# Summing the per-partition counts of a bisection by a round trip through HBM instead of a TensorE product

## Chip, core and metric

One NeuronCore of one Trainium2 chip runs the whole program in one launch. The metric is the device time in microseconds (us); lower is better. The core has five instruction streams: TensorE (PE in the profile, its weight loads PEld), VectorE (DVE), ScalarE (ACT), GpSimd (POOL) and SyncE (SP), which here issues nearly all DMAs.

## The reference

For four sequences of 512 tokens by 512 features, a mask of the 5120 largest entries of a gated softmax is added to x, and the result goes through one transformer block.

```
# per sequence: g = 4, n = 512, k = 5120
adj = emb_s * emb_t * softmax(x) / sqrt(n);  diagonal = -inf
out = zeros; out[top_k(adj.flat, 5120)] = 1;  x = x + out
# block: adaptive layer norm, 16 heads of 128, out projection, gated add,
#        adaptive layer norm, 512 -> 2048 gelu -> 512, gated add
x = x + block(x, cond)
```

## The kernel before

The sequences run one after another (`sequence(b)`, b = 0 to 3); weights are streamed from HBM as pairs of a high and a low part, so that each product is three matmuls (`mm3`, L1395 to L1397).

The top-k threshold of sequence b+1 is found while sequence b runs. It is a bisection of 32 steps (`STEPS`). In each step DVE (`count`, L1027) and ACT (`topk_count`, L778) each count, in every partition, how many of half the elements lie above the candidate `cand`. The two counts of a partition are the two columns of `counts` (128x2, float16). They have to be summed over the 128 partitions, and the sum has to reach every partition. `take_total` does this on PE: one matmul of `counts` with a 128x128 matrix of ones, into a PSUM bank (L1411). DVE then moves the candidate (`topk_move`: L1094, L1097, L1099). A step needs the step before it.

The first `HEAD_STEPS` = 11 steps of a bisection stand in the attention heads: the counts of step s are made in head 4+s, and `topk_move` of step s stands in head 5+s, right behind the four row maxima of that head (L1217) and ahead of the softmax sums, the float16 halves of the probabilities (`halves`, L1236) and the q and k of the next head (`qk_part`, L1187). The other 21 steps stand between the wide products of the block ("out", "mlp_in", "mlp_out"; `between`, `step_at`). The bisection for the first sequence (t = 0) runs alone at the start, and the last sequence has none beside it, so 33 steps lie in heads: 11 in each of the sequences 0, 1 and 2.

A head on PE: 12 matmuls of scores (L1511; they wait for `q_lo` and `k_lo`, DVE's results), the total, 24 matmuls of the next head's q and k, 12 of a v tile (or a part of the out projection), 12 of `attend` for the head before. With the total in bank 6, which `attend` uses too, PE waits for `o_lo` ahead of the total, and for `cand_ready` ahead of `attend`.

The probabilities are turned by four DMA transposes per head, issued on SP (`turn`, L537), each of which waits for `p16_lo` (DVE's L1236), and widened by POOL (L740). SP's queue in heads of the sequences 1 and 2 is: the four transposes of head h, then in head 3 and 7 two halves of v weights (in head 11 two of the out projection), then the q and k weights of head h+3, 1 MB each (`load_split`, L466). In sequence 0 (`first_sequence`) SP issues after each `turn` one raw half of weights and one split half to be stored, three of each in the heads 3, 7 and 11 (`load_raw`, L449 and L441). ACT and POOL split the raw halves.

Of the kernel before, what the change touches and what calls it, by code (L numbers as in the profile page):

```python
# [34 lines left out]
F32 = mybir.dt.float32  # L35
# [4 lines left out]
F16 = mybir.dt.float16  # L40
# [4 lines left out]
P = 128  # L45
# [183 lines left out]
def block_kernel(nc, x, cond, weights, ada_w, cols, out):  # L229
    ctx = ExitStack()  # L230
    with ctx:
        here = [(nc.sbuf_base + 31) // 32 * 32]

        def at(name, shape, dt, offset):
            return nc.alloc_sbuf_tensor_at(name, shape, dt, offset=offset)
# [7 lines left out]
        def new(name, shape, dt):  # L243
            n = 4 if dt in (F32, F32R, I32) else 2
            for s in shape[1:]:
                n *= s
            return at(name, shape, dt, room(n))
# [36 lines left out]
        passed_s = at("passed_s", [P, FIRST_S], BF16, passed_at)  # L284
        gate_t = at("gate_t", [B * 2 * C, P], F32, passed_at)
        small = new("small", [P, NCOLS], F32)
        ident = new("ident", [P, P], F32)
# [24 lines left out]
        offset = new("offset", [P, 1], F16)  # L312
        counts = new("counts", [P, 2], F16)
        cnt_v, cnt_s = counts[:, 0:1], counts[:, 1:2]
        sign_sum = new("sign_sum", [P, 1], F16)
# [19 lines left out]
        scratch = nc.dram_tensor("split_weights", (NHALF, P, 2, HALF), F32, kind="Internal").ap()  # L335

        gate_rows = nc.dram_tensor("gate_rows", (B * 2 * C, P), F32, kind="Internal").ap()
        by_rows = weights[unit_half(8, 0):unit_half(8, 0) + 8].rearrange("(u j) p n -> j p u n", j=2)
# [7 lines left out]
        def sem(name):  # L346
            return ctx.enter_context(nc.semaphore(name))
# [24 lines left out]
        xmax_ready, xexp_done, adj_ready, diag_done = (sem("xmax_ready"), sem("xexp_done"),  # L372
                                                       sem("adj_ready"), sem("diag_done"))
        cand_ready, counted_v, counted_s, total_ready = (sem("cand_ready"), sem("counted_v"),
                                                         sem("counted_s"), sem("total_ready"))
# [57 lines left out]
        def _(sp):  # L433
# [96 lines left out]
            def turn(b, h):  # L530

                k = b * H + h
                for i in range(NT):
                    if k:
# [4 lines left out]
                        .then_inc(turned_in[i], 16)  # L539

            def first_sequence():
                load_raw(2, AHEAD + 2)
# [11 lines left out]
                for h in range(H):  # L554
                    turn(0, h)
                    if h == H - 1:
                        load_x_again(1)
                    load_raw(at + 2, at + 2 + len(first_splits(h)))
                    at += len(first_splits(h))
# [17 lines left out]
            def sequence(b, last=False):  # L577
# [7 lines left out]
                for h in range(2, H):  # L585
                    if h >= 3:
                        turn(b, h - 3)
                    if h % QUAD == 2 and h < 14:
                        load_v(b, h // QUAD + 1)
                    if h == 14:  # L590
                        load_unit(b, 0)
                    load_qk(b, h)
                turn(b, H - 3)
                load_unit_half(b, 1, 0)
                turn(b, H - 2)
                load_unit_half(b, 1, 1)
                load_unit_half(b, 2, 0)
                turn(b, H - 1)
# [420 lines left out]
        def _(dve):  # L1019
# [64 lines left out]
            def topk_move(t, step):  # L1084
                dve.wait_ge(total_ready, t * STEPS + (step + 1))


                bit = TOP_BIT / (1 << step % LEVEL)
                if is_t0(t):
                    move = V.tensor_scalar(cand[:, :], total(step)[:, 0:1], bounds[:, 0:1], bounds[:, 1:2],  # L1090
                                           ALU.max, ALU.min)
                else:
                    bit *= unit(step)
                    V.tensor_scalar(step_up[:, :], total(step)[:, 1:2], 0.5, float(KTOP - P * NCOUNT // 2) - 0.5,  # L1094
                                    ALU.mult, ALU.add)
                    dve.drain()
                    V.tensor_scalar(step_up[:, :], total(step)[:, 0:1], step_up[:, :], bit, ALU.is_gt, ALU.mult)  # L1097
                    dve.drain()
                    move = V.tensor_scalar(cand[:, :], cand[:, :], step_up[:, :], -bit / 2, ALU.add, ALU.add)  # L1099
# [292 lines left out]
        def _(pe):  # L1392
# [111 lines left out]
            def head(b, h, last):  # L1504
# [4 lines left out]
                for i in range(NT):  # L1509
                    rows = slice(i * P, (i + 1) * P)  # L1510
                    mm3(bank[i][:, :], qk[:, 0, 0, rows], qk[:, 0, 1, rows], qk[:, 1, 0, :], qk[:, 1, 1, :],  # L1511
                        True, True).then_inc(scores, 1)
                step = h - FIRST_TOTAL
                if 0 <= step < HEAD_STEPS and not last:
                    pe.wait_ge(o_lo, b * H + h)
                    take_total(b + 1, step)
                if h + 1 < H:
# [9 lines left out]
                if h:  # L1527
                    attend(b, h - 1, step if not last else -1)

            def attend(b, h, step):  # L1530

# [3 lines left out]
                pe.wait_ge(o_lo, b * H + (h + 1))  # L1535
                if 0 <= step < HEAD_STEPS:
                    pe.wait_ge(cand_ready, (b + 1) * (STEPS + 1) + (step + 2))
                pe.wait_ge(widened, (b * H + h + 1) * NT)
# [121 lines left out]
            def sequence(b, first=False, last=False):  # L1660
# [18 lines left out]
                wide(b, "out", 0, KC - 2, KC - 1, y_done)  # L1679
                attend(b, H - 1, -1)  # L1680
                wide(b, "out", 2, 0, 3, y_done)
# [105 lines left out]
```

## Time and profile before

| | us |
|---|---|
| median of 3 runs | 1551.48 |
| lowest, highest | 1547.79, 1551.97 |
| the profiled execution: time | 1549.28 |
| the profiled execution: span of its trace | 1547.5 |

The span is the time from the first to the last instruction of the program; 1.8 us of the profiled execution lie around it. Busy time in the profile counts a matmul from its start to its modelled end, so that neighbouring matmuls overlap; the distance from one start to the next tells what a matmul costs.

### The profile page before, as it was taken

What the parts mean: (1) busy time and instruction counts of PE and PEld (TensorE: products, weight loads), DVE (VectorE), ACT (ScalarE), POOL (GpSimd) and SP (SyncE); (2) the same over time, 40 slices, a digit from 0 to 9 for tenths busy, and PEclk for the clock granted to TensorE, in tenths of its full rate; (3) what the DMA queues carried; (4) which work ended last, traced back from release to release, by engine and by line L of the source; (5) the groups of instructions that cost most, each with busy time, mean ns of one, the idle gap of its engine ahead of it and who ended that gap; (6) DMA issues with size and microseconds to landing.
All of it is one profiled execution on the core that took longest, in us unless ns stands there. A gap on an engine that the chain in (4) does not pass through costs nothing.

```text
span 1547.5 us, 22147 instructions
## 1 busy us (share of the span) xinstructions
PE 1499.1 (97%) x7157; PEld 1244.7 (80%) x7157; DVE 1107.3 (72%) x2572; ACT 884.3 (57%) x1631; POOL 424.2 (27%) x371
## 2 busy tenths in 40 slices
PE   1999999999999999999999999999999999999998
PEld 1878788879788888888878887888878888888987
DVE  7878887777796887876784887876786666664431
ACT  4656777765846566662753666663572655554340
POOL 6714555554021422331000432232000232223000
PEclk9999999999999999999999999999999999999999
DMA  7866899996767677775465788686465686776463
GB/s 293 300 265 191 230 225 267 255 250 241 257 247 246 172 198 202 207 188 182 172 225 217 196 208 197 155 215 206 164 232 190 191 218 160 196 214 158 182 238 118
DMA packets 338611, 327.65 MB, mean 212 GB/s; under 512 B 274848, under 2 KB 279104, under 8 KB 335424
## 3 DMA queue, kind: packets, MB, share of 16 engines
q1 hardware_dynamic: 338208, 325.91, 71.0%
q8 instruction: 57, 0.93, 0.2%
q14 instruction: 58, 0.48, 0.1%
q10 hardware_dynamic: 288, 0.33, 0.1%
HBM read 204.54 MB, written 54.54 MB: 167 GB/s over the span
## 4 chain that ended last, share of the span: by engine, by line
PE 90%; DVE 4%; DVEq 1%; DMA 1%; ACT 1%; issue 1%; SPq 1%; POOL 0%; ACTq 0%; POOLq 0%
PE bank L1395 27%; PE bank L1397 27%; PE bank L1396 27%; PE bank L1717 2%; PE bank L1615 1%; PE bank L1610 1%; PE bank L1611 1%; DVE tb L1027 1%; PE bank L1427 1%; DVEq L1218 1%; DMA w<-split_weights 1%; SPq L537 1%; PE bank L1449 1%; PE bank L1446 1%; PE bank L1445 1%
## 5 line engine op out<-in xcount | busy, mean ns | idle before, releaser
L740 POOL CAST probT<-turned 128x1024 fp32r<-128x1024 f16 x256 | 260.1, 1053 | 679.5 <-PE bank L1397 355.0
L1395 PE MATMUL bank<-xT,w 128*128 128x512 f32 x704 | 279.7, 397 | 0.0
L1396 PE MATMUL bank<-xT,w 128*128 128x512 f32 x704 | 273.9, 389 | 0.0
L1397 PE MATMUL bank<-xT,w 128*128 128x512 f32 x704 | 273.8, 389 | 0.0
L883 ACT ACTIVATE prob<-bank,nbias 128x512 f32<-128x512 f32 x256 | 176.2, 689 | 107.9 <-DVE nbias L1219 98.8
L1236 DVE SCALAR_TENSOR_TENSOR halves<-prob,rinv,halves 128x512 f16<-128x512 f32 x256 | 176.0, 750 | 27.2 <-ACT halves L890 27.2
L890 ACT ACTIVATE halves<-prob,rinv 128x512 f16<-128x512 f32 x256 | 163.8, 712 | 30.6 <-DVE rinv L1232 23.9
L1217 DVE TENSOR_REDUCE rowmax<-bank 128x1 f32<-128x512 f32 x256 | 174.4, 681 | 0.0
L1397 PEld LDWEIGHTS bank<-xT,w 128*128 128x128 f32 x704 | 132.2, 188 | 28.0
L1395 PEld LDWEIGHTS bank<-xT,w 128*128 128x128 f32 x704 | 132.9, 189 | 25.0
L1396 PEld LDWEIGHTS bank<-xT,w 128*128 128x128 f32 x704 | 132.4, 188 | 24.9
L660 POOL TENSOR_TENSOR w<-wraw,w 128x1024 fp32r<-128x1024 f32 x38 | 94.0, 2478 | 178.8 <-ACT w L819 177.6
L1395 PE MATMUL bank<-act,w 128*128 128x512 f32 (+1 forms) x320 | 113.4, 354 | 0.0
L1397 PE MATMUL bank<-act,w 128*128 128x512 f32 (+1 forms) x320 | 111.0, 347 | 0.0
L1396 PE MATMUL bank<-act,w 128*128 128x512 f32 (+1 forms) x320 | 111.0, 347 | 0.0
L778 ACT ACTIVATE passed_s<-adj,cand 128x1024 bf16<-128x1024 uint16 (+1 forms) x64 | 73.8, 1153 | 62.5 <-DVE cand L1099 37.4
L1187 DVE SCALAR_TENSOR_TENSOR act<-bank,small,act 128x512 fp32r<-128x512 f32 x64 | 47.9, 748 | 85.4 <-ACT act L910 85.4
L910 ACT ACTIVATE act<-bank,small 128x512 fp32r<-128x512 f32 x64 | 44.0, 688 | 106.3 <-PE bank L1397 106.3
L778 ACT ACTIVATE passed_s<-low,cand 128x1024 bf16<-128x1024 f32 (+1 forms) x64 | 74.0, 1156 | 51.0 <-DVE cand L1099 24.1
L1395 PE MATMUL bank<-qk 128*128 128x512 f32 x256 | 100.1, 391 | 1.7 <-DVE qk L1187 1.2
L1395 PE MATMUL bank<-w,act 128*128 128x512 f32 x256 | 101.5, 397 | 0.0
L1187 DVE SCALAR_TENSOR_TENSOR qk<-bank,small,qk 128x512 fp32r<-128x512 f32 x128 | 90.2, 744 | 14.2 <-ACT qk L875 7.9
(171 smaller groups left out, 3314.7 us busy)
## 6 DMA issues: line engine op xcount, KB each, us to landing
w<-split_weights SPq DMA_DIRECT2D x154, 1024.0 KB, 5.6
split_weights<-w SPq DMA_DIRECT2D x38, 1024.0 KB, 6.8
wraw<-weights_in SPq DMA_DIRECT2D x48, 512.0 KB, 4.8
split_weights<-xT SPq DMA_DIRECT2D x7, 1024.0 KB, 8.0
adaw<-ada_w_in SPq DMA_DIRECT2D x4, 1536.0 KB, 13.0
xr<-x_in SPq DMA_DIRECT2D x4, 1024.0 KB, 5.7
turned<-halves SPq DMA_TRANSPOSE x256, 3.3
split_weights<-qk SPq DMA_DIRECT2D x3, 1024.0 KB, 7.6
```

Source lines behind the costliest of these rows:

```text
L660: nc.gpsimd.tensor_tensor(w[:, region, 1, span], wraw[:, k % 2, :], w[:, region, 0, span].bitcast(F32), ALU.subtract)\
L740: nc.gpsimd.tensor_copy(probT[:, :, :, i * P:(i + 1) * P].rearrange("p a j t -> p (a j) t"), turned_of(h)[:, i, :, :]).then_inc(widened, 1)
L778: nc.scalar.activation(passed_s[:, :2 * NCOUNT - at], src, ACT.Sign, bias=cand[:, :], scale=-1.0, accum_out=cnt_s[:, :]).then_inc(counted_ ...
L883: nc.scalar.activation(prob[:, i, :], bank[i][:, :], ACT.Exp, bias=nbias[:, i:i + 1], scale=SCALE, accum_out=rowsum[:, i:i + 1]).then_inc( ...
L890: nc.scalar.mul(halves_of(h)[:, i, 0, :], prob[:, i, :], rinv[:, i:i + 1]).then_inc(p16_hi, 1)
L910: nc.scalar.activation(act[:, 0, h, :], bank[6][:, :], ACT.Identity, bias=col("bv", h))\
L1187: return V.scalar_tensor_tensor(dst, src, bias, hi.bitcast(F32), ALU.add, ALU.subtract)
L1217: V.reduce_max(rowmax[:, i:i + 1], bank[i][:, :], AX.X)
L1236: V.scalar_tensor_tensor(halves_of(h)[:, i, 1, :], prob[:, i, :], rinv[:, i:i + 1], halves_of(h)[:, i, 0, :], ALU.mult, ALU.subtract).then ...
L1395: pe.matmul(dst, w_hi_ap, x_hi_ap, start=first, stop=False)
L1396: pe.matmul(dst, w_hi_ap, x_lo_ap, start=False, stop=False)
L1397: return pe.matmul(dst, w_lo_ap, x_hi_ap, start=False, stop=last)
```

## The change

In heads, PE takes no total. SP stores `counts` as 128 rows of two numbers in HBM, waits until the store has landed, and loads the 256 numbers into every partition (`all_counts`). DVE adds them up (`summed`) and moves the candidate from these sums. PE's waits that belonged to the total in bank 6 go with it. The steps outside heads, and the bisection at the start, stay as they were.

```
+        all_counts = at("all_counts", [P, P, 2], F16, passed_at)
+        summed = new("summed", [P, 2], F32)
+        count_rows = nc.dram_tensor("count_rows", (P, 2), F16, kind="Internal").ap()
...
+            def exchange_counts(t, h):
+                step = h + 1 - FIRST_TOTAL
+                if not 0 <= step < HEAD_STEPS:
+                    return
+                done = 16 * ((t - 1) * HEAD_STEPS + step + 1)
+                wait_apart(sp, counted_v, t * STEPS + step + 1)
+                wait_apart(sp, counted_s, t * STEPS + step + 1)
+                sp.dma_start(count_rows, counts[:, :]).then_inc(counts_out, 16)
+                wait_apart(sp, counts_out, done)
+                sp.dma_start(all_counts[:, :, :].rearrange("p n c -> p (n c)"),
+                             count_rows.rearrange("n c -> (n c)").unsqueeze(0).to_broadcast([P, 2 * P]))\
+                    .then_inc(counts_in, 16)
...
                 for h in range(H):
                     turn(0, h)
+                    exchange_counts(1, h)
...
                     load_qk(b, h)
+                    if h >= 3 and not last:
+                        exchange_counts(b + 1, h - 3)
                 turn(b, H - 3)
                 load_unit_half(b, 1, 0)
+                if not last:
+                    exchange_counts(b + 1, H - 3)
                 turn(b, H - 2)
                 load_unit_half(b, 1, 1)
+                if not last:
+                    exchange_counts(b + 1, H - 2)
...
             def topk_move(t, step):
-                dve.wait_ge(total_ready, t * STEPS + (step + 1))
+                if is_t0(t):
+                    dve.wait_ge(total_ready, step + 1)
+                    sums = total(step)
+                elif step < HEAD_STEPS:
+                    dve.wait_ge(counts_in, 16 * ((t - 1) * HEAD_STEPS + step + 1))
+                    V.tensor_reduce(summed[:, :], all_counts[:, :, :].rearrange("p n c -> p c n"), AX.X, ALU.add)
+                    dve.drain()
+                    sums = summed
+                else:
+                    dve.wait_ge(total_ready, t * (STEPS - HEAD_STEPS) + step + 1)
+                    sums = total(step)
...
-                step = h - FIRST_TOTAL
-                if 0 <= step < HEAD_STEPS and not last:
-                    pe.wait_ge(o_lo, b * H + h)
-                    take_total(b + 1, step)
...
-                if 0 <= step < HEAD_STEPS:
-                    pe.wait_ge(cand_ready, (b + 1) * (STEPS + 1) + (step + 2))
```

SP's queue in sequence 1, before, from the transposes of head 6 to those of head 8:

```order
L537 DMA_TRANSPOSE turned_0_71<-halves_0_69 128x8x128 [waits widened,p16_lo] x4
L466 DMA w<-split_weights 128x2x1024 [waits k_done]
L537 DMA_TRANSPOSE turned_0_71<-halves_0_69 128x8x128 [waits widened,p16_lo] x4
L466 DMA w<-split_weights 128x2x1024 [waits v_done] x2
L466 DMA w<-split_weights 128x2x1024 [waits k_done]
L537 DMA_TRANSPOSE turned_0_71<-halves_0_69 128x8x128 [waits widened,p16_lo] x4
```

The same stretch after the change (its transposes are L541, its weight loads L470):

```order
L541 DMA_TRANSPOSE turned_0_71<-halves_0_69 128x8x128 [waits widened,p16_lo] x4
L470 DMA w<-split_weights 128x2x1024 [waits k_done]
L553 DMA count_rows<-counts 128x2 [waits counted_v,counted_s]
L555 DMA all_counts<-count_rows 128x256 [waits counts_out]
L541 DMA_TRANSPOSE turned_0_71<-halves_0_69 128x8x128 [waits widened,p16_lo] x4
L470 DMA w<-split_weights 128x2x1024 [waits v_done] x2
L470 DMA w<-split_weights 128x2x1024 [waits k_done]
L553 DMA count_rows<-counts 128x2 [waits counted_v,counted_s]
L555 DMA all_counts<-count_rows 128x256 [waits counts_out]
L541 DMA_TRANSPOSE turned_0_71<-halves_0_69 128x8x128 [waits widened,p16_lo] x4
```

The store and the load of the counts stand behind the weight loads of the same head, one or three of them, and ahead of the next head's transposes.

DVE's stream, before, from the last row maximum of head 5 in sequence 0 to the reciprocal of the softmax sums:

```order
L1217 TENSOR_REDUCE rowmax<-bank 128x1 [waits scores]
L1219 TENSOR_SCALAR nbias<-rowmax 128x1
L1094 TENSOR_SCALAR step_up<-bank 128x1 [waits total_ready]
L1097 TENSOR_SCALAR step_up<-bank,step_up 128x1
L1099 TENSOR_SCALAR cand<-cand,step_up 128x1
L1230 TENSOR_SCALAR rowsum<-rowsum 128x1 [waits exp_done]
L1230 TENSOR_SCALAR rowsum<-rowsum 128x1
L1232 RECIPROCAL rinv<-rowsum 128x2
```

The same place after the change (L1251 and L1253 are the row maximum and its bias):

```order
L1251 TENSOR_REDUCE rowmax<-bank 128x1 [waits scores]
L1253 TENSOR_SCALAR nbias<-rowmax 128x1
L1115 TENSOR_REDUCE summed<-all_counts 128x2 [waits counts_in]
L1128 TENSOR_SCALAR step_up<-summed 128x1
L1131 TENSOR_SCALAR step_up<-summed,step_up 128x1
L1133 TENSOR_SCALAR cand<-cand,step_up 128x1
L1264 TENSOR_SCALAR rowsum<-rowsum 128x1 [waits exp_done]
L1264 TENSOR_SCALAR rowsum<-rowsum 128x1
L1266 RECIPROCAL rinv<-rowsum 128x2
```

One instruction is added, and the wait at this place is for the load on SP's queue.

## Rows read from the trace of the kernel before

**Rows 1.** The page: busy time of each engine.

```profile
PE 1499.1 (97%) x7157; PEld 1244.7 (80%) x7157; DVE 1107.3 (72%) x2572; ACT 884.3 (57%) x1631; POOL 424.2 (27%) x371
```

**Rows 2.** Timeline of PE, sequence 1, head 8: start us, us, instruction.

```profile
593.57 0.39 PE L1397 MATMUL bank<-qk 128*128 128x512 f32 x1
593.80 0.18 PE L1411 MATMUL bank<-counts,ones 128*128 128x2 f16 x1
...
594.16 0.39 PE L1396 MATMUL bank<-xT,w 128*128 128x512 f32 x1
...
604.81 0.39 PE L1395 MATMUL bank<-qk 128*128 128x512 f32 x1
```

**Rows 3.** Timeline of DVE, sequence 1, heads 5, 8, 9 and 15.

```profile
555.72 0.15 DVE L1094 TENSOR_SCALAR step_up<-bank 128x1 f32<-128x1 f32 x1
...
595.99 0.15 DVE L1094 TENSOR_SCALAR step_up<-bank 128x1 f32<-128x1 f32 x1
...
598.14 2.74 DVE L1236 SCALAR_TENSOR_TENSOR halves<-prob,rinv,halves 128x512 f16<-128x512 f32 x4 [0.20 <-ACT halves L890]
600.80 1.41 DVE L1187 SCALAR_TENSOR_TENSOR qk<-bank,small,qk 128x512 fp32r<-128x512 f32 x2
...
603.52 0.09 DVE L1027 DVE_READ_ACCUMULATOR tb<-adj,cand 128x1 f16 x1
...
610.29 0.15 DVE L1094 TENSOR_SCALAR step_up<-bank 128x1 f32<-128x1 f32 x1
...
690.08 0.15 DVE L1094 TENSOR_SCALAR step_up<-bank 128x1 f32<-128x1 f32 x1
```

**Rows 4.** Timeline of SP's issues (SPq), sequence 1: behind heads 7 and 9.

```profile
591.25 2.69 SPq L466 DMA_DIRECT2D w<-split_weights  x3
...
613.30 5.55 SPq L537 DMA_TRANSPOSE turned<-halves  x4
618.97 0.54 SPq L466 DMA_DIRECT2D w<-split_weights  x1
```

**Rows 5.** DMA issues of the whole span: count, size, median us to landing.

```profile
w<-split_weights SPq DMA_DIRECT2D x154, 1024.0 KB, 5.6
...
turned<-halves SPq DMA_TRANSPOSE x256, 3.3
...
small<-cols_in ACTq DMA_DIRECT2D x1, 64.0 KB, 1.8
```

**Rows 6.** Weight loads (L466) from 591.1 to 606 us; a DMA issue at 99 us.

```profile
DMA to landing us min/median/max: 5.4/6.7/10.0
...
gate_rows<-gate_t SPq DMA_DIRECT2D x1, 16.0 KB, 5.9
```

**Rows 7.** Timeline of SP's issues, sequence 0, heads 4 and 5.

```profile
185.12 9.17 SPq L537 DMA_TRANSPOSE turned<-halves  x4
194.34 0.58 SPq L449 DMA_DIRECT2D wraw<-weights_in  x1
...
204.18 0.60 SPq L449 DMA_DIRECT2D wraw<-weights_in  x1
```

**Rows 8.** Timeline of DVE, sequence 0, head 5.

```profile
193.78 0.15 DVE L1094 TENSOR_SCALAR step_up<-bank 128x1 f32<-128x1 f32 x1
...
197.15 2.90 DVE L1236 SCALAR_TENSOR_TENSOR halves<-prob,rinv,halves 128x512 f16<-128x512 f32 x4 [1.73 <-ACT halves L890]
```

**Rows 9.** Timeline of DVE and PE, sequence 1, step 11 in the out projection.

```profile
696.57 0.09 DVE L1027 DVE_READ_ACCUMULATOR tb<-adj,cand 128x1 f16 x1
...
698.23 0.18 PE L1411 MATMUL bank<-counts,ones 128*128 128x2 f16 x1
```

**Rows 10.** Timeline of PE at 87 and 91 us, and one window's busy time and granted clock.

```profile
86.49 3.76 PE L1723 MATMUL bank<-w 128*128 128x512 f32 x8
...
90.63 5.63 PE L1723 MATMUL bank<-w 128*128 128x512 f32 x24
...
90.00:1547.00 1457.00, 1445.91 (x6859) 1194.89 (x6857) 1034.24 (x2381) 833.51 (x1551) 366.61 (x324) 1.00 0.71 206
```

More of the change, by code:

```diff
@@ L373, in block_kernel @@
                                                        sem("adj_ready"), sem("diag_done"))
+        counts_out, counts_in = sem("counts_out"), sem("counts_in")
         cand_ready, counted_v, counted_s, total_ready = (sem("cand_ready"), sem("counted_v"),
@@ L1084, in topk_move @@
             def topk_move(t, step):
-                dve.wait_ge(total_ready, t * STEPS + (step + 1))
+                if is_t0(t):
[9 more added lines that the diff above has]
+                    sums = total(step)
                 bit = TOP_BIT / (1 << step % LEVEL)
                 if is_t0(t):
-                    move = V.tensor_scalar(cand[:, :], total(step)[:, 0:1], bounds[:, 0:1], bounds[:, 1:2],
+                    move = V.tensor_scalar(cand[:, :], sums[:, 0:1], bounds[:, 0:1], bounds[:, 1:2],
                                            ALU.max, ALU.min)
@@ L1093, in topk_move @@
                     bit *= unit(step)
-                    V.tensor_scalar(step_up[:, :], total(step)[:, 1:2], 0.5, float(KTOP - P * NCOUNT // 2) - 0.5,
+                    V.tensor_scalar(step_up[:, :], sums[:, 1:2], 0.5, float(KTOP - P * NCOUNT // 2) - 0.5,
                                     ALU.mult, ALU.add)
                     dve.drain()
-                    V.tensor_scalar(step_up[:, :], total(step)[:, 0:1], step_up[:, :], bit, ALU.is_gt, ALU.mult)
+                    V.tensor_scalar(step_up[:, :], sums[:, 0:1], step_up[:, :], bit, ALU.is_gt, ALU.mult)
                     dve.drain()
@@ L1527, in head, with attend @@
                 if h:
-                    attend(b, h - 1, step if not last else -1)
-            def attend(b, h, step):
+                    attend(b, h - 1)
+            def attend(b, h):
                 q, m = h // QUAD, h % QUAD
@@ L1679, in sequence @@
                 wide(b, "out", 0, KC - 2, KC - 1, y_done)
-                attend(b, H - 1, -1)
+                attend(b, H - 1)
                 wide(b, "out", 2, 0, 3, y_done)
```

## The prediction

> **What bounds the kernel now.** I read the page first, then PE's timeline through one head, then DVE's and SP's for the same head. PE is busy 97% of the span [rows 1], and in a head of sequence 1 its matmuls start 0.227 us apart without a hole: the last score matmul at 593.57, the total at 593.80, and the scores of the next head at 604.81 [rows 2]. So PE is the bound, and another engine matters only when it lets PE run dry. The total itself costs PE little: the second matmul behind it starts at 594.16 where 593.57 + 2 x 0.227 = 594.02 would do, 0.13 to 0.14 us [rows 2].
>
> DVE is the closest behind. In the same head the move is at 595.99, the halves follow from 598.14, q and k of the next head end at 602.21 (600.80 + 1.41), and the new count is read at 603.61 [rows 3]. PE takes the scores that wait for q and k at 604.81 [rows 2]: a slack of 2.6 us. The next move is at 610.29 [rows 3]. From one move to the next is 13.4 us on average, 134.36 us for the ten from 555.72 to 690.08 [rows 3]. Counted from a move: +2.9 the first half is ready (598.14 + about 0.75), +6.2 q and k, +7.6 the counts.
>
> **What the change removes.** 33 totals of 0.13 us, 4.3 us, and PE's waits for bank 6, which cost nothing in a stream without holes. The gain counts only as long as PE stays the bound in heads.
>
> **What it adds: a new loop.** The counts leave DVE at +7.6, but the store stands in SP's queue behind the four transposes and the weight load of the head. Behind head 9 the transposes are issued from 613.30 for 5.55 us and the load at 618.97 [rows 4]; against the move at 610.29 [rows 3] that is +3.0, +8.6 and +8.7. A 1 MB load lands 5.6 us (median) after its issue [rows 5], at +14.3. Where three loads follow the transposes they are issued from 591.25 to 593.94 [rows 4], and the longest landing time in that stretch is 10.0 us [rows 6], that of the third: its issue at about 592.5 plus 10.0 is 602.5. A head of 60 matmuls and a total is 60 x 0.2267 + 0.13 = 13.73 us, so the move ahead of these loads was at 595.99 - 13.73 = 582.3, so it lands at +20.3.
>
> Does the store wait for these loads? Everything goes through one queue of SP. The three loads, issued within 2.7 us, have landing times from 5.4 to 10.0 us in their stretch, and the little store of 16 KB (`gate_rows`), issued right behind the loads of the next x and cond, took 5.9 us [rows 6], while a 64 KB load on a free queue took 1.8 [rows 5]. So I take it that a small DMA lands just behind what stands ahead of it: 0.4 us behind (the bounds are 0.1 and 1.5; a store to HBM of 4 bytes a partition has no row). SP wakes and issues the load: 0.1. The load of 64 KB in 512-byte rows: 2.2 (from 1.8 by the free 64 KB load to 3.3 by a transpose, which moves small pieces too). DVE wakes and adds: the row maximum over 512 columns takes 0.68 and a single column 0.15, so 256 columns about 0.42, with its drain 0.5.
>
> Together 3.2 us behind the landing: a move follows the one before by 14.3 + 3.2 = **17.5 us with one load, 20.3 + 3.2 = 23.5 us with three**. The loop closes on itself, since the next halves, transposes, load and store all count from the late move. It is longer than PE's head, so PE goes dry ahead of the scores, 3.8 or 9.8 us a head.
>
> Here a page is weighed against the rows. The row says 1.8 us for 64 KB on a free queue [rows 5]. The Trainium skill, "DMA: Bandwidth & Descriptors", section "Anatomy of one DMA", gives about 2.0 us as the fixed part of one DMA, and with it alone a round trip would be about 4 us and the change nearly free. The same page's section "Queues, rings and completion order" says that each engine consumes the descriptors of a ring in order, which is what the landing times above show, and which speaks against the change.
>
> **The sum for sequences 1 and 2.** Of the eleven exchanges the first follows head 4. Its move is at about 541.9 (555.72 less 13.73), so that the move of head 5 comes 17.5 later, near 559.4 instead of 555.72. Of the ten after it, eight have one load and two (heads 7 and 11) have three: 8 x 17.5 + 2 x 23.5 = 187 us. The move of head 15 is then at 746.4 instead of 690.08, 56.3 us late. Step 11 follows between matmuls of the out projection: its count is read at 696.66 and PE comes for it at 698.23 [rows 9], so 1.6 us of the lateness are hidden, and 54.7 us reach PE. Behind that PE is solid again and nothing is given back. Two sequences: 109 us.
>
> **Sequence 0** is different: the exchange stands ahead of the raw loads, behind transposes alone. A transpose lands 3.3 us after its issue [rows 5], the fourth at +10.6, so that a move comes at 10.6 + 3.2 = 13.8, no later than now. But SP now sits in the wait for 2 to 3 us, and the raw halves and stores start that much later and run into the next transposes (those of head 5 needed 198.15 to 204.18 = 6.0 us already [rows 7]): I take 1 us for each of eight heads. In heads 4, 8 and 12, behind the triple loads, the transposes end late: those of head 4 at 194.29 [rows 7], past the move at 193.78 [rows 8]. The move would come at 194.3 + 2.1 + 0.1 + 2.2 + 0.6 = 199.3, 5.5 late; DVE lost 1.73 of it anyway, waiting for ACT ahead of the halves [rows 8]: 3.8 net, three times 11.4. For the raw halves that ACT needs in heads 7 and 11, 3 us in all. Together 22 us (bounds 8 and 50).
>
> **Sum:** 109 + 22 = 131 us, on the profiled execution's 1549.3 us: 1680 us. The median of the runs is 1551.5, 2 us above it, so I predict 1681. The gain of 4.3 us is not subtracted, since PE is no longer the bound there.
>
> **The rivals.**
> (a) *The store does not wait for the weights* (it overtakes them or shares the engines). For it: loads are not in flight for the whole head. Against: the 5.9 us of the 16 KB store [rows 6]. Then the store lands near +11.4 and a move comes after 14.2 us (one load) or 15.6 (three): 0.8 a head on average over the 13.4, near 9 us a sequence, with some 15 to 20 in sequence 0: about 1587 us.
> (b) *The round trip is wholly hidden and PE gains.* The load would have to land before the row maxima end, near +13.1, that is within 4.4 us of the weight load's issue at +8.7. Only then are the 4.3 us of the totals left: 1547 us. The weight load alone takes 5.6 [rows 5]; very unlikely.
> (c) *PE's clock falls in the new holes and stays down.* The granted clock is 1.00 from 90 us to the end, where PE idles 11 of 1457 us; ahead of that, after small matmuls only, eight matmuls took 3.76 us, and later 24 took 5.63 [rows 10]: 0.43 us each against 0.23, the levels 1.2 and 2.4 GHz. Should a hole of 4 or 10 us bring the low level for a few microseconds, some ten matmuls cost 0.2 more each, 2 us, inside the 3.8 us that PE waits anyway: nothing. If it stays for whole heads, 60 matmuls take 25.6 us, over the 17.5, 8 more in nine heads of two sequences at least: about 1830 us. The Trainium skill, "TensorE: Matmul & The Clock Gate", section "What's actually happening", says that the low clock is the state without activity and that sustained activity lifts it; by that rule the holes could bring the low clock, but busy stretches of 13.6 us would lift it.
> (d) *The store or the broadcast is slow* (all partitions read the same 512 bytes; 4-byte pieces are written): 5.3 instead of 3.2 us behind the landing adds 2.1 in 33 heads, 69 us: 1750 us.
>
> **How the numbers follow.** The forecast has 0.70, (a) 0.13, (b) 0.02, (c) 0.03, (d) 0.12. Within the forecast the bounds of the tail (2.4 to 4.3 us instead of 3.2) give 22 x 0.8 + 14 = 32 us less and 22 x 1.1 + 28 = 52 more: 1649 to 1733. The range reaches towards (a), which is one in eight, and takes in part of (d): 1625 to 1740. A measurement of this kernel tells about 0.3%, 4.7 us, from no change. Faster by more needs (b) and more: 0.02. Within: (b)'s remainder and a mild (a): 0.03. Slower: 0.95.
>
> **What the new profile would show.** In heads 5 to 15 of the sequences 1 and 2, DVE's sum waits for the load of the counts, moves are 17 to 18 us apart, twice 23 to 24; PE waits ahead of the scores for DVE's q and k, 3 to 4 us a head and about 10 after heads 7 and 11; the store lands just behind the weight load. Heads of sequence 3, and everything after the heads, last as before. The prediction is wrong if the store lands within 2 us of its issue while weights are under way, if the load takes far more than 2 us, or if PE's matmuls are 0.43 us apart for whole heads.

## The result and the profile after

The changed kernel takes 1926.66 us (median of 4 runs, 1918.91 to 1931.53) against 1549.63 before (4 runs): a ratio of 1.243, 95% interval 1.238 to 1.248. The direction of the forecast was right and its size was not: 131 us were forecast, 377 measured, and the time lies far outside the range of 1625 to 1740.

The page of the changed kernel begins as follows, with the lines that answer to [rows 1]; its profiled execution took 1931.53 us.

```profile
span 1929.8 us, 22270 instructions
...
PE 1574.3 (82%) x7124; PEld 1297.9 (67%) x7124; DVE 1125.0 (58%) x2605; ACT 879.9 (46%) x1631; POOL 426.9 (22%) x371
...
PE   3999566667999965666599997667569999999999
...
PEclk9999778778999978787799998878779999999999
...
DMA count_rows<-counts 17%; PE bank L1429 13%; PE bank L1430 13%; PE bank L1431 13%; SPq L541 10%; DMA all_counts<-count_rows 7%; DVE halves L1270 2%; PE bank L1745 2%; ACT halves L915 2%; DVEq L1252 1%; DVE tb L1052 1%; PE bank L1643 1%; PE bank L1638 1%; SPq L470 1%; PE bank L1639 1%
```

PE is no longer solid: its row has three troughs, in the heads of the sequences 0, 1 and 2, and the granted clock dips at the same places. The first entry of the chain that ended last is now the store of the counts, 17% of the span or about 330 us; the load has 7%. Sequence 3, which has no exchange, ends the row at 9s as before.

The chain of waits names the loop:

```profile
DVE summed L1115 <- DMA all_counts<-count_rows: 386.4, 33, 16.5
...
PE bank L1429 <- DVE qk L1221: 272.0, 30, 14.4
```

The three numbers are the idle time in all, how often, and the longest. All 33 sums wait, 11.7 us each on average, and PE then waits for DVE's q and k in 30 heads. From the score matmuls' starts in the two traces the loss can be placed by stage (us, from the scores of head 4 to those of head 15, and from there to the first head of the next sequence, in sequence 3 to the end):

| | heads 4 to 15, before | after | rest, before | after |
|---|---|---|---|---|
| sequence 0 | 152.5 | 263.6 | 159.6 | 171.8 |
| sequence 1 | 148.9 | 265.4 | 159.3 | 174.7 |
| sequence 2 | 150.1 | 260.2 | 159.5 | 175.5 |
| sequence 3 | 147.6 | 147.6 | 142.6 | 142.6 |

The heads lose 337.7 us and the stretches behind them 43.6, together 381 of the 382.3 us between the two spans. Of the 43.6, 29.1 are three waits of PE for the count of step 11, and about 13 are matmuls that start late behind these waits (the clock, below).

SP's and DVE's timelines of one head (sequence 1, head 9; the sum ahead of it started at 791.29, and the first instruction of the move stands 0.5 us behind a sum) show the loop that stood in [rows 3, 4] before:

```profile
794.79 6.29 SPq L541 DMA_TRANSPOSE turned<-halves  x4
801.19 0.54 SPq L470 DMA_DIRECT2D w<-split_weights  x1
801.92 0.45 SPq L553 DMA_DIRECT2D count_rows<-counts  x1
812.38 0.32 SPq L555 DMA_DIRECT2D all_counts<-count_rows  x1
...
816.36 0.42 DVE L1115 TENSOR_REDUCE summed<-all_counts 128x2 f32<-128x256 f16 x1 [11.93 <-DMA all_counts<-count_rows]
```

The weight load of 801.19 takes 5.3 us and lands at 806.5, 14.7 us behind the move, close to the +14.3 of the forecast. The store lands 5.8 us after it, at 812.3, and the load 4.0 us after its own issue. A move follows the one before by 25.1 us here and by about 24 in most heads; 17.5 were forecast.

While SP waits for that store, the DMA engines stand still. Two stretches of this head, with the busy time of PE, PEld, DVE, ACT and POOL, the granted clock, the busy share of the 16 DMA engines and GB/s:

```profile
801.90:806.50 4.60, 4.60 (x19) 3.70 (x19) 2.02 (x6) 2.73 (x8) 2.03 (x2) 0.85 0.80 257
806.80:812.20 5.40, 5.40 (x26) 4.47 (x25) 0.00 (x0) 0.00 (x0) 0.00 (x0) 1.00 0.00 0
```

The store's packets are gone with the last ones of the weights, before 806.5, and for 5.4 us the DMA engines carry nothing: what is missing is only the word that the store has landed.

Over the whole span the two DMAs have these landing times (us min/median/max, L553 and then the medians of both):

```profile
DMA to landing us min/median/max: 7.1/9.4/14.3
...
all_counts<-count_rows SPq DMA_DIRECT2D x33, 64.0 KB, 4.4
...
count_rows<-counts SPq DMA_DIRECT2D x33, 0.5 KB, 9.4
```

In sequence 0 nothing but transposes stands ahead of the store, and it is as slow: issued at 217.94, and SP issues the dependent load at 226.47.

```profile
217.94 0.44 SPq L553 DMA_DIRECT2D count_rows<-counts  x1
226.47 0.32 SPq L555 DMA_DIRECT2D all_counts<-count_rows  x1
```

### The profile page after: what moved, and what is told of

The parts are those of the page before. It is cut to its first block, busy times and chain, and to the rows that moved or that the text cites. A ratio compares the mean times of both kernels' runs of the same rounds, so it can differ in the third digit from the quotient of the medians.

```text
span 1929.8 us, 22270 instructions
## 1 busy us (share of the span) xinstructions
PE 1574.3 (82%) x7124; PEld 1297.9 (67%) x7124; DVE 1125.0 (58%) x2605; ACT 879.9 (46%) x1631; POOL 426.9 (22%) x371
## 4 chain that ended last, share of the span: by engine, by line
PE 46%; DMA 25%; SPq 11%; DVE 9%; issue 3%; ACT 3%; DVEq 2%; POOL 0%; ACTq 0%; POOLq 0%
DMA count_rows<-counts 17%; PE bank L1429 13%; PE bank L1430 13%; PE bank L1431 13%; SPq L541 10%; DMA all_counts<-count_rows 7%; DVE halves L1270 2%; PE bank L1745 2%; ACT halves L915 2%; DVEq L1252 1%; DVE tb L1052 1%; PE bank L1643 1%; PE bank L1638 1%; SPq L470 1%; PE bank L1639 1%
## 5 line engine op out<-in xcount | busy, mean ns | idle before, releaser
L1429 PE MATMUL bank<-qk 128*128 128x512 f32 x256 | 128.6, 502 | 272.0 <-DVE qk L1221 272.0
L1429 PEld LDWEIGHTS bank<-qk 128*128 128x128 f32 x256 | 62.5, 244 | 297.8 <-DVE qk L1221 283.8
L1115 DVE TENSOR_REDUCE summed<-all_counts 128x2 f32<-128x256 f16 x33 | 13.9, 420 | 386.4 <-DMA all_counts<-count_rows 386.4
L1251 DVE TENSOR_REDUCE rowmax<-bank 128x1 f32<-128x512 f32 x256 | 174.7, 682 | 7.5 <-PE bank L1431 6.2
L1430 PE MATMUL bank<-qk 128*128 128x512 f32 x256 | 122.9, 480 | 0.0
L1431 PE MATMUL bank<-qk 128*128 128x512 f32 x256 | 121.2, 474 | 0.0
L1429 PE MATMUL bank<-act,w 128*128 128x512 f32 (+1 forms) x320 | 116.7, 365 | 0.0
L1430 PE MATMUL bank<-act,w 128*128 128x512 f32 (+1 forms) x320 | 114.2, 357 | 0.0
L1431 PE MATMUL bank<-act,w 128*128 128x512 f32 (+1 forms) x320 | 113.7, 355 | 0.0
## 6 DMA issues: line engine op xcount, KB each, us to landing
adaw<-ada_w_in SPq DMA_DIRECT2D x4, 1536.0 KB, 13.5
```

The costliest lines, as they stand in the source:

```text
L1251: V.reduce_max(rowmax[:, i:i + 1], bank[i][:, :], AX.X)
L1429: pe.matmul(dst, w_hi_ap, x_hi_ap, start=first, stop=False)
L1430: pe.matmul(dst, w_hi_ap, x_lo_ap, start=False, stop=False)
L1431: return pe.matmul(dst, w_lo_ap, x_hi_ap, start=False, stop=last)
```

## The experiments

Theory A, formed from these rows: the store of 512 bytes in 128 pieces of 4 bytes is slow by itself, wherever it is issued, and the load has a price of its own. Theory B: both are slow because of what stands ahead of them in SP's queue (the forecast's own reason, only larger). Theory C: the clock that falls in PE's holes costs the time.

**e1: small DMAs alone.** A program that issues each kind of DMA six times on SP and waits for each.

```
+ alone(sp.dma_start(dense, counts[:, :]))                 # L55: 128 pieces of 4 bytes, one stretch of 512
+ alone(sp.dma_start(gap64[:, 0:2], counts[:, :]))         # L57: the same, 64 bytes apart
+ alone(sp.dma_start(wide64, row64[:, :]))                 # L61: 64 bytes a partition
+ alone(sp.dma_start(got[:, :], every))                    # L69: one row of 512 bytes to all partitions
+ alone(sp.dma_start(got[:, :], wide512))                  # L71: 128 different rows of 512 bytes
```

> No part of the block is computed: this program only issues small DMAs on SP, one at a time, each awaited, six of each kind, and fills the output with ones. Theory A (the store of 128 pieces of 4 bytes into one stretch of 512 bytes of HBM is slow by itself): about 7 us from issue to landing on the empty queue, near the 7.5 us that the store took in sequence 0 of the changed kernel, and about 2 us for stores of 64 or 512 bytes a partition. If pieces that fall into the same line hinder each other, 4-byte pieces 512 bytes apart take far less, 2 to 3 us; if the small piece itself costs, they take 7 as well. Theory B (the store waits for transposes and weights ahead of it in the queue): 2 to 2.5 us for every store here. For the load of one 512-byte row into all partitions: theory A 3.3 to 4.4 us against 2 for a load of 128 different rows; theory B 2 us for both.

Timeline of SP; each row is six DMAs from the first issue to the last, so that the next row's start less this one's, divided by six, is one DMA with its wait:

```profile
6.14 41.06 SPq L55 DMA_DIRECT2D dense<-counts  x6
55.20 7.32 SPq L57 DMA_DIRECT2D gap<-counts  x6
63.60 7.31 SPq L59 DMA_DIRECT2D gap<-counts  x6
72.00 7.35 SPq L61 DMA_DIRECT2D wide<-row  x6
...
109.51 14.60 SPq L69 DMA_DIRECT2D got<-dense  x6
126.61 9.28 SPq L71 DMA_DIRECT2D got<-wide  x6
```

(55.20 - 6.14) / 6 = 8.2 us for the dense store on an empty queue; (63.60 - 55.20) / 6 = 1.4 us for the same pieces 64 bytes apart, and 1.4 for 64 bytes a partition. Theory B fails for the store: nothing is ahead of it here. The small piece is not the cause either, its neighbourhood is. One row into all partitions takes 2.8 us, 128 different rows 1.8 (the next row starts at 137.35).

Where the 8.2 us go, the DMA engines show. Stretches of the first dense store: us, POOL's busy time, granted clock, busy share of the DMA engines, GB/s:

```profile
6.14:7.20 1.06, 0.00 (x0) 1.00 0.07 1
7.20:13.40 6.20, 0.00 (x0) 1.00 0.00 0
```

All its packets have passed 1.0 us after the issue, as those of the spaced store have; the other 6.3 us go by before the landing is told, with idle DMA engines. So the pieces hinder each other after the DMA engines have sent them; where and how, no run here shows.

**e8: how dense is too dense.** The same program with rows 64, 32, 16 and 8 bytes apart.

> No part of the block is computed: small DMAs alone, one at a time, six of each kind. Stores of 4 bytes a partition with rows 64, 32, 16 and 8 bytes apart and dense. Theory A1 (what collides is a stretch of 64 bytes): 1.4 us at 64, and at 32 bytes (two pieces in a stretch) a little more, at 16 and 8 bytes more yet, 7 to 8 us dense. Theory A2 (only the dense row is special): 1.4 us down to 8 bytes. The load of one row into all partitions right behind a fast store of that row (512 bytes from one partition): 4.5 us if a fresh row is slow, 2.8 us if it was the slow store that made it so; a load of 128 different rows: 1.8 us.

Timeline of SP, the spacings in that order, then dense:

```profile
6.15 7.33 SPq L57 DMA_DIRECT2D gap<-counts  x6
14.57 7.33 SPq L59 DMA_DIRECT2D gap<-counts  x6
22.98 9.56 SPq L61 DMA_DIRECT2D gap<-counts  x6
34.05 18.79 SPq L63 DMA_DIRECT2D gap<-counts  x6
56.53 44.42 SPq L65 DMA_DIRECT2D dense<-counts  x6
```

By the same division: 1.4, 1.4, 1.8, 3.7 and 8.8 us (the row behind the last starts at 109.43). From 16 bytes down, each halving of the distance doubles the time; at 32 bytes nothing is left of it, so a stretch of 64 bytes as the thing that collides (A1) is not what shows, rather one of 32 or so. A load of one row right behind a fast store of that row took 2.8 us in every round, no more than the load of an old row: freshness costs nothing. Behind the dense store the load took 3.2 to 4.9 us in e1. There its first packet moves 1.3 to 3.1 us after its issue, against 1.0 on a free queue, and the packets then pass in the usual 1.5 us: the store holds up what comes right behind it, even when its landing has been told.

**e2: no exchange at all**, the sum on DVE kept.

```
-                sp.dma_start(count_rows, counts[:, :]).then_inc(counts_out, 16)
-                wait_apart(sp, counts_out, done)
-                sp.dma_start(all_counts...).then_inc(counts_in, 16)
-                    V.tensor_reduce(summed[:, :], all_counts[:, :, :].rearrange("p n c -> p c n"), AX.X, ALU.add)
+                    V.tensor_reduce(summed[:, :], counts[:, :].unsqueeze(2).to_broadcast([P, 2, P]), AX.X, ALU.add)
```

> Leaves out the store and the load of the counts; the sum on DVE adds the partition's own two counts 128 times, so the threshold is not the right one, with the same instructions. Both theories: all the time comes back, and the 33 totals that PE no longer takes give 33 x 0.13 = 4.3 us besides: 1545 us, ratio to the kernel before 0.997. If the added sum on DVE (0.42 us) or the removed waits of PE mattered, it would lie 10 us or more above 1550.

1545.57 us (10 runs) against 1549.41, ratio 0.9973, 0.9964 to 0.9983. So everything but the two DMAs together is a gain of 3.8 us: PE's 33 totals (4.3 us by [rows 2]) are worth about what the rows said, though by the stages of the two traces none of it comes in sequence 0 (152.7 and 159.5 us against 152.5 and 159.6), and the sum on DVE is free as long as DVE has its slack.

**e3: the load alone.**

```
-                sp.dma_start(count_rows, counts[:, :]).then_inc(counts_out, 16)
-                wait_apart(sp, counts_out, done)
+                sp.dma_start(all_counts...bitcast(F32), cond[0:1, 0:P].to_broadcast([P, P])).then_inc(counts_in, 16)
```

> Leaves out the store; the load takes 512 bytes of cond into every partition, and the sum on DVE adds the partition's own counts, so the threshold is not the right one. Theory A: the load costs its 4 to 6 us and, in sequences 1 and 2, comes behind the weight load: moves 17 to 18 us apart in these and about 15 in sequence 0, about 1640 us. If nothing waited for the weight load, moves would be 14 us apart there and the time 1570 us. Theory B (everything slow sits in the queue ahead of the store): 1640 as well, with a landing of the load 2 us behind that of the weights.

1628.03 us, ratio 1.051 (1.049 to 1.053). In sequences 1 and 2 the load's landing follows that of the weights ahead of it by about 0.2 us in 19 of 22 cases (4.7 to 6.3 us after its issue behind one load, 8.5 to 9.1 behind three), in sequence 0 it takes 4.4 us behind the transposes. So the load does as the forecast said of small DMAs: it lands just behind the weights that stand ahead of it, and never sooner. Moves behind one load of weights are about 15 us apart, not the 17 to 18 of the expectation.

**e4: the store alone.** DVE waits for `counts_out`.

> Leaves out the load; DVE waits for the landing of the store and adds the partition's own counts, so the threshold is not the right one. Theory A: the store keeps its 7.5 us in sequence 0 and 9.5 us behind one weight load, so moves are about 18 us apart in sequence 0 and 19.7 in sequences 1 and 2: about 1930 - 33 x 4.7 = 1775 us. Theory B (a store that lands with what is ahead of it once the load's share is gone): moves 15 us apart, 1600 us.

1790.29 us, ratio 1.155 (1.153 to 1.157), near theory A's 1775. The store takes 9 us in sequence 0 and lands some 5 us behind the weights in the others.

**e5: the round trip with rows 64 bytes apart.**

```
-        count_rows = nc.dram_tensor("count_rows", (P, 2), F16, kind="Internal").ap()
+        count_rows = nc.dram_tensor("count_rows", (P, 32), F16, kind="Internal").ap()
-                sp.dma_start(count_rows, counts[:, :]).then_inc(counts_out, 16)
+                sp.dma_start(count_rows[:, 0:2], counts[:, :]).then_inc(counts_out, 16)
```

> The whole round trip, but each partition's 4 bytes go to a row of their own, 64 bytes apart in HBM, and the load takes 512 bytes of cond instead of them; the sum on DVE adds the partition's own counts, so the threshold is not the right one. Theory A (pieces of one dense stretch hinder each other, 7 to 8.8 us against 1.4 us spaced, measured alone): the store lands within 0.5 us of the weights ahead of it, moves are 17.5 to 18 us apart with one load of weights, and the time is about 1700 us, near the 1681 of the forecast. Theory D (in the kernel the store is slow for another reason, such as the traffic beside it): it stays near 1900 us.

1715.67 us, ratio 1.107 (1.105 to 1.109). DMA issues, median us to landing:

```profile
all_counts<-cond_in SPq DMA_DIRECT2D x33, 64.0 KB, 2.8
...
count_rows<-counts SPq DMA_DIRECT2D x33, 0.5 KB, 4.9
```

The store now lands 0.2 us behind the weights (bound of the forecast: 0.1 to 1.5), the load takes 2.8, and moves behind one load of weights are 18 us apart. For the sequences 1 and 2 this is the kernel that the forecast described. In sequence 0 the store takes 1.9 us, but the load 4.2: there the raw loads are issued 0.4 us behind it, and its packets pass beside theirs in 2.9 us instead of 1.5. Both DMAs are faster at once (4.4 to 2.8 for the load), as in e1.

**e12: the true sum without 4-byte pieces.** DVE turns the counts in blocks of 32 partitions, the store has rows of 64 bytes.

```
+                V.transpose(turned_counts[:, :], padded[:, :]).then_inc(counts_turned, 1)
+                sp.dma_start(count_rows, turned_counts[:, :]).then_inc(counts_out, 16)
...
+                             count_rows.rearrange("(b n) c -> b (n c)", b=4)[:, 0:64].unsqueeze(0).to_broadcast([P, 4, 64]))\
```

> A round trip with the true sum and without pieces of 4 bytes: DVE turns the counts within blocks of 32 partitions, so that each partition stores one row of 64 bytes and the counts stand in eight of these rows; the load takes four pieces of 128 bytes for each partition. Theory A (dense 4-byte pieces are what makes the store slow and the load behind it slower): as e5, the store 0.2 us behind the weights, moves 18 us apart, plus about 1 us a move for the turn on DVE and a load in 512 pieces of 128 bytes: 1716 + 33 = 1750 us, against 1927 of the changed kernel. If it was the missing dependence of e5's load on the stored rows (there the load read other memory) that made e5 fast, it stays above 1850 us.

1722.79 us, ratio 1.112 (1.110 to 1.114), with the sum that the kernel needs: 204 us below the changed kernel, at the cost of one more DVE instruction, and 27 us below the 1750 of the expectation. The load of the rows just stored takes 3.3 us, so it was not the missing dependence that made e5 fast. It does not beat the kernel before.

**e6: the exchange ahead of the weight loads.**

```
                     if h >= 3:
                         turn(b, h - 3)
+                        if not last:
+                            exchange_counts(b + 1, h - 3)
```

> The changed kernel with the exchange ahead of the weight loads of the head instead of behind them, the sum unchanged. Theory A: the store still takes its 7.5 us, as in sequence 0; only the queue's share goes: moves 23 us apart in sequences 1 and 2 as in sequence 0 instead of 24.2, and in the two heads with three loads too instead of 28.9: 2 x (9 x 1.2 + 2 x 5.9) = 45 us less, 1880 us. Theory B (the weights ahead of the store are the cause): moves about 16 us apart, below 1750 us.

1912.15 us, ratio 1.234 (1.232 to 1.235): 14.5 us below the changed kernel, not the 45 expected. The changed kernel's own four runs lie 12.6 us apart, so this gain is small, though the two intervals do not meet. The store takes 8.3 us, and the load, with the weights now issued right behind it, rises:

```profile
all_counts<-count_rows SPq DMA_DIRECT2D x33, 64.0 KB, 5.8
```

The weights behind the load are not what makes it slow. In e5's head 14 weights are issued 0.5 us behind the load as well, and it takes 2.9 us. The packets tell more. In e6 the first one of the load moves 2.8 us (median) after its issue in the sequences 1 and 2, against 1.0 in e5; a load issued at 712.92 in sequence 1 has idle DMA engines at first (the engines and columns are those of the stretches above):

```profile
712.92:715.80 2.88, 2.88 (x15) 2.37 (x14) 0.00 (x0) 0.00 (x0) 0.00 (x0) 1.00 0.00 0
```

The weight loads behind it take 8.1 to 8.3 us (medians of the two sequences) instead of 5.6 to 5.7. So the dense store delays whatever is issued right behind it. Behind the weights about 3 of its 8 us were hidden, since it landed 5 us after them; ahead of them none is. Sequence 0, where nothing was moved, took 6 us more in this execution.

**e9 and e10: the exchange issued by ACT**, behind its own count, with spaced rows (e9) and with the dense store and the true sum (e10).

```
+                    if h + 1 < H:
+                        exchange_counts(b + 1, h + 1 - FIRST_TOTAL)    # on act_e
```

> The round trip of e5 (4-byte pieces 64 bytes apart, the load from cond, the sum of the partition's own counts, so not the right threshold), issued by ACT right behind its count instead of by SP, so that it stands behind no transposes and no weights in a queue. If the queue ahead is what is left of the loss, the chain is 7.6 + 0.5 + 1.9 + 0.1 + 2.8 + 0.5 = 13.4 us behind a move, inside the 13.7 of a head: 1550 to 1565 us. If DMAs of ACT's queue share the 16 engines with the transposes and the weights under way and so take as long as behind them, moves stay 16 to 18 us apart: 1630 to 1715 us.

> The changed kernel, sum unchanged, with its dense store and its load issued by ACT right behind its count. Theory A (the dense store costs 7 to 9 us wherever it is issued): 7.6 + 0.5 + 8.3 + 0.1 + 4.6 + 0.5 = 21.6 us from move to move, 33 x 2.4 = 80 us below the changed kernel, about 1850 us. Theory B (the weights and transposes ahead are the cause): at most 15 us a move, below 1620 us.

e9: 1667.23 us, ratio 1.076 (1.075 to 1.078); e10: 1896.79, ratio 1.224. DMA issues of e9, then of e10:

```profile
all_counts<-cond_in ACTq DMA_DIRECT2D x33, 64.0 KB, 4.8
...
count_rows<-counts ACTq DMA_DIRECT2D x33, 0.5 KB, 2.4
```

```profile
all_counts<-count_rows ACTq DMA_DIRECT2D x33, 64.0 KB, 5.6
...
count_rows<-counts ACTq DMA_DIRECT2D x33, 0.5 KB, 9.4
```

Out of SP's queue the spaced store takes 2.4 us, but the load 4.8 where it takes 2.8 alone and in e5. The first expectation of e9 (1550 to 1565 us) failed; the second gave the time and the distance (moves 16 to 17 us apart behind one load), though the store did not take as long as behind the weights. A queue of its own does not let the load pass: in 15 of the 22 heads of the sequences 1 and 2 it lands 0.2 us behind the weights, which SP had mostly issued 1 to 2 us earlier, and its first packet moves 3.4 us (median) after its issue, when those of the weights are nearly through. ACT waits for the store meanwhile, some 4 us a head.

In e10 the dense store keeps its 9.4 us on a queue that holds nothing else, which settles theory B for the store inside the kernel too. It also slows SP's queue, on which it does not stand: the weight loads there take 13.4 us (median, sequences 1 and 2), against 5.7 in e9. My 1850 was 47 us low: the store took 9.4 us where I had put 8.3, the load 5.6 where I had put 4.6.

**e11: the load of 128 different rows**, otherwise as e3.

> As e3 (no store, the partition's own counts are summed), but the load takes 128 different rows of 512 bytes of x instead of one row 128 times. Alone, 128 different rows took 1.8 us and one row 2.8. If that 1 us carries over, 1628 - 33 x 1 = 1595 us; if the landing is set by the weights ahead of it in sequences 1 and 2 (0.2 us behind them in e3), only the 11 moves of sequence 0 gain: 1617 us.

1614.49 us against 1628.03 of e3: 13.5 us less, 10.8 of them in the heads of sequence 0. There the load itself falls from 4.4 to 2.1 us, but only 1 us a move comes back, since most moves are then 13 to 14 us apart, PE's own head. Where the weights set the landing, one row for all partitions costs little.

**e7: PE kept busy in the holes.** 28 more matmuls of 512 columns ahead of the scores and of step 11.

```
+                if FIRST_TOTAL <= h + 1 < H and not last:
+                    pe.wait_ge(exp_done, b * (H * NT) + (h + 1) * NT)
+                    keep_busy()
```

> The changed kernel with 28 more matmuls of 512 columns (6.4 us at the high clock) on PE in each hole ahead of the scores and of step 11, their results unused. Theory A (the low clock costs next to nothing in heads, since PE waits for the loop anyway, and 2.2 us behind each of the three holes ahead of step 11): 1927 - 3 x 2.2 = 1920 us. Theory C (the clock that falls in the holes is a major part of the loss): 50 us or more less, below 1880 us.

The mean granted clock rises from 0.908 to 0.964, and the time does not fall: 1945.46 us, 19 us more than the changed kernel. Theory C, which forecast 50 us less, fails. The test is partial, since matmuls that start late (0.33 to 0.52 us behind the one before) fall from 318 to 209 and not to none. But what DVE and SP do in the loop does not quicken with the clock: behind one load of weights the transposes are issued 3.5 us after the sum both in the changed kernel (0.908) and in e5 (0.960). DVE's sums wait as long as before (382.7 us), and the stretch behind the heads shortens by 0.2, 0.5 and 2.8 us. In the traces the heads take 18 us more. In each sequence the batch ahead of the scores of head 5, where there is no hole yet, costs 6.3 to 6.6 us, which the heads behind it give back for the most part; and the 66 DMAs of the exchange take 15 us more in sum than in the changed kernel's trace. Why they do is not shown.

## Why the forecast was wrong

**What bounds the kernel, and what the change removes: right.** The totals are priced at 0.13 us each, and with no exchange the kernel gains 3.8 us of the 4.3 (e2).

**The loop: right.** The count goes from DVE through SP's queue into HBM and back to DVE, it closes on itself, and it is longer than PE's head. The end of the transposes' issue at +8.6 and the landing of one weight load at +14.3 came as read from [rows 4, 5] (8.7 and 14.3 in most heads of the changed kernel); where three loads stand ahead, the last lands 19.0 to 20.3 us after the move in e5 (+20.3 forecast) and up to 23.5 in the changed kernel. A DMA that does not collide lands just behind the weights ahead of it (e3, e5: 0.2 us).

**The step that failed: the tail behind the landing, "Together 3.2 us".** It has four terms. Waking SP and the sum on DVE were right (the sum takes 0.42). The store, taken at 0.4 us behind the weights with bounds of 0.1 to 1.5, is about 5; the load, taken at 2.2 with bounds of 1.8 to 3.3, is about 4.2. With 0.1 for waking SP and 0.5 for the sum and its start, the tail is 5.0 + 0.1 + 4.2 + 0.5 = 9.8 us, and 14.3 + 9.8 = 24.1 us is the distance between moves that is measured. These 6.6 us too many, 22 times over, are 145 of the 149 us by which the forecast missed the sequences 1 and 2; sequence 0 missed by 101. The range had no room for it: its upper tail of 4.3 us is even less than the upper bounds of its own terms add up to, 1.5 + 0.1 + 3.3 + 0.5 = 5.4, which by the same sum would give 1757 us. That, too, is far below 1927. Of the signs of being wrong that I had set, the load came (4.4 us where 2 was the mark); for a slow store I had set none.

The cause of the term, shown by e1, e8, e5 and e12: 128 pieces of 4 bytes in one stretch of 512 bytes hinder each other. The store needs 8.2 to 8.8 us alone, and 1.4 with rows 32 bytes apart. I had no row for such a store, said so, and yet gave it an upper bound of 1.5, with a store of 32 rows of 512 bytes as the nearest row (`gate_rows`, [rows 6]), which has no small pieces. The Trainium skill's page "DMA: Bandwidth & Descriptors" says in its section "Specifications" that transfers under 512 bytes are read, changed and written; it gives no price. If that alone were the cost here, pieces of 4 bytes would be as slow 64 bytes apart as dense, and they take 1.4 against 8.2 us: in these runs density costs, not size. The 2.0 us that the prediction quoted from the Trainium skill's section "Anatomy of one DMA" are given there for DMAs issued by GpSimd; on SP's queue a small spaced store takes 1.4 us and a 64 KB load 1.8 to 2.8 (e1). No term of the sum used them.

**Sequence 0: wrong by the same terms.** I set it apart with 22 us since only transposes stand ahead of its store. But the dense store lasts longer than a weight load, so it hardly matters what stands ahead of it: 111 us in heads and 12 behind them. Without the collision, e5 has 38.7 and 4.4 there, still twice my 22: moves are 15.5 us apart where I had 13.8, since the load takes 4.2 us and not 2.2. One row for all partitions is what costs there: 128 different rows take 2.1 (e11).

**The ladder of the loss**, each step by its run: 1545.6 with neither DMA (e2), 1628.0 with the load (e3), 1715.7 with a store that doesn't collide (e5), 1926.7 with the dense one. So 82 us belong to the load and the queue ahead of it, 88 to the store, which the load must now wait for, even when it doesn't collide, and 211 to the collision, with the slower load that comes with it. Without those 211 the forecast of 1681 would have been 35 us low, 21 of them in sequence 0.

**The rivals.** (a) failed: in SP's queue nothing overtakes the weights (its 0.8 us a head should have been 1.1 by its own distances, 9 x 0.8 and 2 x 2.2 over eleven, which adds some 2 us to its 1587); (b) failed, and e9 shows why even a queue of its own does not bring it: the load still lands behind the weights, 4.8 us after its issue. (d), a slow store and a slow broadcast, is what happened, with 6.6 us instead of the 2.1 that I had allowed; I had it at 0.12, with no row for the store and a transpose as the upper bound of the load. (c) happened in its mild form, and its price of nothing was right for the heads; behind them, where it had not looked, the clock costs about 13 us. PE's timeline after a hole of 8.8 us:

```profile
823.17 0.77 PE L1429 MATMUL bank<-qk 128*128 128x512 f32 x1 [8.81 <-DVE qk L1221]
823.73 0.63 PE L1430 MATMUL bank<-qk 128*128 128x512 f32 x1
824.16 0.63 PE L1431 MATMUL bank<-qk 128*128 128x512 f32 x1
...
827.39 0.40 PE L1430 MATMUL bank<-qk 128*128 128x512 f32 x1
827.63 0.39 PE L1431 MATMUL bank<-qk 128*128 128x512 f32 x1
```

The scores start 0.43 us apart, the level of 1.2 GHz, and from 827.4 on 0.23 to 0.24 apart, that of 2.4. In the windows of this stretch the granted clock is 0.66 while PE idles, 0.80 over the next 9.8 us and 1.00 behind that:

```profile
814.00:823.10 9.10, 0.36 (x2) 0.00 (x0) 5.72 (x16) 4.84 (x9) 0.00 (x0) 0.66 0.34 47
823.20:833.00 9.80, 9.80 (x35) 7.98 (x36) 5.54 (x12) 4.07 (x10) 4.17 (x4) 0.80 0.69 176
833.50:837.00 3.50, 3.50 (x17) 2.89 (x16) 0.00 (x0) 0.00 (x0) 0.00 (x0) 1.00 0.00 0
```

The Trainium skill, "TensorE: Matmul & The Clock Gate", section "What's actually happening", has it so: without activity the clock is low, and sustained activity lifts it; this trace agrees. 318 matmuls of the changed kernel start some 0.2 us late, 63 us in all. 254 of them lie in heads, where PE waits for the loop anyway, and 64 behind the heads, where they add to the time; e7 took a third of them away and gained nothing.

## What to carry to other kernels

A round trip through HBM in a serial loop costs the landings of everything ahead of it in its queue, and then two DMAs; its place in the queue is priced by the landing time of the neighbours, not by its own size. Another queue did not help the load here: it landed behind the weights under way on SP's. A store of a few bytes a partition must not be packed: turn or pad the data so that each piece has at least 32 bytes to itself, and take the price of such a store from a store of the same shape, not of the same number of bytes. Where no row has the shape, the upper bound is not a bound; a small program that issues the DMA alone gives it in one run.

## What the hardware showed that I had not expected

Stores of 128 pieces of 4 bytes to HBM, alone: 1.4 us with rows 64 or 32 bytes apart, 1.8 at 16, 3.7 at 8, 8.2 to 8.8 dense (e1, e8). The packets of the dense store have passed 1.0 us after its issue; for the rest of its time the DMA engines are idle (e1). A load right behind the dense store takes 3.2 to 4.9 us instead of 2.8, and the weight loads of SP's queue take 13.4 us instead of 5.7 while the dense store runs on ACT's (e10, e9). One 512-byte row loaded into all 128 partitions takes 2.8 us, 128 different rows 1.8. On ACT's queue, beside the weights of SP's, the 64 KB load takes 4.8 us and lands 0.2 us behind them in 15 of 22 heads; on SP's, issued when the weights have landed, 2.8 (e9, e5).
